# LoRA residual kernel on one Trainium2 core: the copy of the split product moves from GpSimd to VectorE

## The reference

```
B_sel = B[adapter_ids]
A_sel = A[adapter_ids]
Bx  = einsum('bni,bri->bnr', x, B_sel)
out = einsum('bnr,bor->bno', Bx, A_sel)
return x + out
```

## Time and profile before

| what | value |
|---|---|
| median of 3 runs | 96.18 us (95.92 to 96.72) |
| profiled execution | 96.29 us, its span 94.4 us |
| mean granted TensorE clock in it | 0.945 of full |
| moved by DMA | 34.83 MB, mean 369 GB/s |

### The profile page before, as it was taken

How to read it: one execution, slowest core, us unless ns; L and a number is a source line. 1 busy time by engine, 2 the same in 40 slices (tenths; PEclk the granted TensorE clock), 3 DMA queues, 4 the chain that set the end, 5 groups by cost and what they waited for, 6 DMA issues and landing times.

```text
span 94.4 us, 3723 instructions
## 1 busy us (share of the span) xinstructions
PE 81.5 (86%) x1472; PEld 64.5 (68%) x1472; DVE 58.4 (62%) x105; ACT 53.1 (56%) x138; POOL 67.1 (71%) x152
## 2 busy tenths in 40 slices
PE   3994999999999999899999999999989999652800
PEld 3993998787786768587877787777767877440400
DVE  0009541219696949396969677685857695949760
ACT  2219687985747475657667676757556757110000
POOL 6003906379798999979797979797979798986000
PEclk9999999999999999999999999999999999975555
DMA  1999999999999999999999999999999998664676
GB/s 19 305 294 394 419 417 408 408 408 412 401 413 406 408 403 403 410 412 403 408 413 408 419 403 415 417 412 415 417 410 419 410 380 327 271 266 198 247 318 252
DMA packets 11202, 34.83 MB, mean 369 GB/s; under 512 B 2866, under 2 KB 2866, under 8 KB 11186
## 3 DMA queue, kind: packets, MB, share of 16 engines
q1 hardware_dynamic: 11040, 34.08, 91.7%
q10 hardware_dynamic: 146, 0.52, 1.6%
HBM read 17.83 MB, written 16.78 MB: 367 GB/s over the span
## 4 chain that ended last, share of the span: by engine, by line
PE 69%; POOL 9%; DMA 7%; issue 5%; DVE 4%; POOLq 2%; DVEq 1%
PE t_bank L221 31%; PE bx_bank L234 18%; PE y_banks L254 16%; POOL a_duo L162 7%; DMA x_all<-in_A 7%; PE y_banks L212 4%; DVE x_all L363 1%; DVE x_all L341 1%; POOL b_duo L151 1%; DVEq L43 1%; DVE x_all L338 1%; DVE x_all L344 1%; POOL bx_parts L169 1%; POOLq L43 0%; POOLq L162 0%
## 5 line engine op out<-in xcount | busy, mean ns | idle before, releaser
L363 DVE TENSOR_TENSOR x_all<-y_banks,x_all 128x1024 f32<-128x1024 f32 x32 | 39.1, 1224 | 18.7 <-PE y_banks L254 18.2
L301 ACT COPY x_t<-t_bank 128x512 f32<-128x512 f32 x64 | 34.4, 591 | 19.5 <-PE t_bank L221 19.5
L162 POOL CAST a_duo<-a_table 128x512 fp32r x64 | 36.6, 609 | 3.4 <-ACT a_table L306 3.2
L221 PE MATMUL t_bank<-ident,x_all 128*128 128x128 f32 x256 | 34.9, 279 | 1.3 <-DMA x_all<-in_x 1.2
L221 PEld LDWEIGHTS t_bank<-ident,x_all 128*128 128x128 f32 x256 | 27.5, 141 | 7.8 <-issue 4.9
L151 POOL COPY b_duo<-b_table 128x256 f32 x64 | 23.2, 403 | 11.1 <-ACT b_table L287 6.2
L254 PE MATMUL y_banks<-a_duo,bx_parts 64*128 64x512 f32 x128 | 20.8, 445 | 4.0 <-POOL bx_parts L169 3.5
L234 PE MATMUL bx_bank<-x_t,b_duo 128*32 128x64 f32 x1024 | 21.7, 222 | 1.1 <-issue 0.6
L234 PEld LDWEIGHTS bx_bank<-x_t,b_duo 128*32 128x32 f32 x1024 | 16.2, 109 | 7.1 <-issue 6.2
L254 PEld LDWEIGHTS y_banks<-a_duo,bx_parts 64*128 64x128 f32 x128 | 12.0, 197 | 7.5 <-issue 3.5
L355 DVE TENSOR_TENSOR bx_parts<-bx_bank,bx_parts 32x64 fp32r<-32x64 f32 x64 | 14.0, 219 | 4.8 <-ACT bx_parts L316 3.7
(11 more groups left out here) (13 smaller groups left out, 7.4 us busy)
## 6 DMA issues: line engine op xcount, KB each, us to landing
out_y<-x_all SPq DMA_DIRECT2D x32, 512.0 KB, 12.4
x_all<-in_x SPq DMA_DIRECT2D x15, 1024.0 KB, 18.8
x_all<-in_x SPq DMA_DIRECT2D x2, 512.0 KB, 6.0
x_all<-in_B ACTq DMA_DIRECT2D x1, 512.0 KB, 4.1
x_all<-in_A SPq DMA_DIRECT2D x1, 512.0 KB, 6.2
id_row<-in_ids ACTq DMA_DIRECT2D x1, 0.2 KB
```

The lines of the kernel that those rows point to most:

```text
L162: last = nc.gpsimd.tensor_copy(a_duo[duo % 2][:, k, :], a_table[:, bass.ds(adapters[k] * BANK, BANK)])
L221: last = nc.tensor.transpose(t_bank[unit % 2][:, c * P:(c + 1) * P], x_all[:, 2 * duo + tile, at:at + P], ident[:, :])
L301: nc.scalar.copy(x_t[duo % 2][:, half * HALF:(half + 1) * HALF, tile, :], t_bank[unit % 2][:, :].rearrange("p (c n) -> p c n", c=HALF)).th ...
L363: nc.vector.tensor_tensor(here, y_banks[tile][:, :], here, ALU.add).then_inc(y_drained, 1)
```

## The change

double_parts is no longer an instruction of GpSimd but of VectorE. There it stands directly behind split_rest of the same duo and ahead of add_x of tile 1, with a wait for rest_done of that duo. Its operands are the same. GpSimd's waits on parts_done and a_gathered go away with it; PE's wait on parts_done in up() stays.

```diff
@@ gpsimd: gather_b @@
                 if duo >= 2:
                     pool.wait_ge(bx_done, duo - 1)
-                    pool.wait_ge(parts_done, duo - 1)
@@ gpsimd: gather_a @@
                 if duo >= 2:
                     pool.wait_ge(y_filled, 2 * (duo - 1))
-                    pool.wait_ge(parts_done, duo)
...
-            def double_parts(duo):
-                pool.wait_ge(rest_done, duo + 1)
-                pool.wait_ge(a_gathered, duo + 1)
-                nc.gpsimd.tensor_copy(own_tokens(duo, K_UP, 2 * K_UP),
-                                      own_tokens(duo, 0, K_UP)).then_inc(parts_done, 1)
...
                 gather_a(duo, here)
-                double_parts(duo)
@@ vector @@
+            def double_parts(duo):
+                dve.wait_ge(rest_done, duo + 1)
+                nc.vector.tensor_copy(own_tokens(duo, K_UP, 2 * K_UP),
+                                      own_tokens(duo, 0, K_UP)).then_inc(parts_done, 1)
...
             split_rest(0)
+            double_parts(0)
             for duo in range(1, DUOS):
                 add_x(duo - 1, 0)
                 split_rest(duo)
+                double_parts(duo)
                 add_x(duo - 1, 1)
```

## The result

The changed kernel takes 95.68 us at the median of 18 runs (94.71 to 97.1) against 96.17 of before; ratio 0.9927, 95% interval 0.9898 to 0.9955. Timed twice more it gave 0.9898 (0.9827 to 0.9969) and 0.9894 (0.9852 to 0.9936). So it is faster by 0.7 to 1.1%, about 0.7 to 1.0 us, and not by the forecast 1.46. By the line of 1% that the prediction drew, the first ratio, 0.9927, is no change (chance 0.30) and not faster (chance 0.60). Some executions are over 1.5% longer than the fastest of their kernel: ratios leave them out, medians and ranges don't, and the profiles of middle_only, after_half_stores and act_double_again are of such an execution. The profiled execution took 95.48 us, its span 93.5 (before 96.29 and 94.4).

What follows compares the result with a forecast made beforehand. No engine is full; order decides, with GpSimd's 4.57 us turn holding PE's 4.34. 0.50 + 0.15 + 0.87 - 0.06 = 1.46 off 96.29 gives 94.8 us; own range 94.0 to 95.3, stated range 94.0 to 96.6.

Steps and rivals of the forecast that it cites:

- the line of 1%: Least change told from none, 0.96 us: faster below 95.2 us (0.60), slower above 97.1 (0.10), same between (0.30).
- GpSimd's turn of 4.57 against PE's 4.34: Duo loop: GpSimd loses 0.23 us a turn and then holds PE; without the copy its turn is about 4.0.
- The two turns held by GpSimd: Middle turns of 4.58 and 4.60 us, where PE waits for GpSimd's copy, fall to 4.34 each: 0.50 us gained.
- U12 to U13: From PE's first weight load of up(12) to that of up(13): 4.49 us before, 0.15 gained.
- The third rival: PE's stops "issue" inside down() grow 0.8 us in all and add in full: 95.6 us, no change; chance 0.15.
- U13 to U14: From PE's first weight load of up(13) to that of up(14): 4.42 us falls to 3.55, 0.87 gained.
- The copy at 0.31 + 0.2: VectorE's new copy per duo: 0.31 us alone, plus 0.2 for disturbance by GpSimd's gathers running beside it.
- Slack of 0.37: Middle turns: add_x tile 1, behind the new copy, still ends 0.37 us before PE needs it, covering the 0.2.
- The one-gather rival: VectorE's copy waits for the running gather each time, 0.41 to 0.57 us: 95.3 to 96.6 us; chance 0.15.
- The batch rival: VectorE's copy waits 0.96 us behind all four a_duo gathers: about 99.5 us, slower; chance 0.10.
- From U14 on nothing changes: Tail from PE's first weight load of up(14): 0.06 us lost up to add_x(14,0), then nothing; clock left at 0.53.
- The low end of the range: Own range's 94.0 us: copy at 0.22 and 0.08 for the unknowns, and some of PE's holds "issue" gone.

Runs made afterwards that it cites:

- middle_only: Changed kernel with the last two copies back on GpSimd, so VectorE copies for duos 0 to 13 only; ratio 0.9898 to the kernel before.
- after_half_stores: Changed kernel with each tile's store writing only its first 512 columns, half of the output left out; 94.08 us, ratio 0.9713.
- act_double_again: Second timing of the version with the copy on ScalarE instead of VectorE, beside the changed kernel; median 95.50 us, ratio 0.9855 to the kernel before.

## Why the prediction was right in its mechanism and too large in its sum

- *GpSimd's turn of 4.57 against PE's 4.34 makes the lag:* right. After, GpSimd waits for PE in 13 turns; taking its gathers away instead of the copy has the same effect.
- *The two turns held by GpSimd, 0.50, and U12 to U13, 0.15:* this is the step that failed: 0.65 was counted in full, and U0 to U13 changed by +0.08. The holds by GpSimd went (turns 8 and 9 lost 0.36, U12 to U13 0.14), but PE's hold in down(12) took 0.29 back, and the one in down(4) grew by 0.23. The third rival, "PE's own holds take it", is what happened: the three holds are longer by 0.6 in all, where it had 0.8. It added longer holds to the time as if they were independent. The point that it missed is that such a hold swallows what is won between its place and the one before it, so the wait for GpSimd ahead of up(10) had hidden part of it.
- *U13 to U14, 0.87:* right in size, 1.07. The 0.2 between them is the 0.2 that I added for gathers beside the copy: duo 14's copy took 0.29.
- *The copy at 0.31 + 0.2:* 0.29 + 0.24 in the middle. Right.
- *Slack of 0.37 covers it:* right, 0.1 left. The one-gather rival had the mechanism: the copy waits for the gather that runs beside it (last section). But it had 0.4 for the wait, and 0.24 was measured, so the slack covered it. The batch rival had 0.96; by its own formula it comes to about 99.7 and not 99.5, a slip that changes nothing.
- *From U14 on nothing changes:* within 0.1. Leaving the time as it was in spite of the clock was right too: PE ran at the full clock there and only 0.09 was gained.
- *The low end of the range:* no. I let it come from holds that might go. In no profile with full stores did the third hold go, and in the three of the changed kernel none did.

Luck has a part in the total. The profiled execution gained 0.81. From U0 to the last addition's end it gained 1.1, and 1.1 and 1.4 in the two further profiles of the changed kernel. The start took 0.36 of it and the end, behind the last addition, gave 0.18 back. One profile alone understates the gain by that.

What is not settled: why the hold in down(4) grew. It is 0.28 before, 0.29 with only the end changed, 0.28 and 0.27 with few gathers, and 0.48 to 0.51 in the five profiles with 24 warm-ups in which DVE copies beside gathers in the middle; with the copy on ScalarE it is 0.38 and 0.44. So it is longest with that overlap. By what way isn't shown.

## What to carry to other kernels

Before a stall is counted as gain, look for the next stop behind it that has another cause: a transfer, or the engine's own instructions. Ask also from where that stop counts its time. Here it ends some 6.4 us after PE passed a fixed place, so it swallowed the gain behind that place and left the gain ahead of it. What is won behind the last such stop counts in full; here only the last two copies moved gave 0.7%, against 0.7 to 1.1% for all sixteen. Two engines on one resource are priced well from the one place in the trace where they already meet. Slack is spent in the order of the waiting engine's own work: once that engine has no idle time, its sum is the turn.

## What the runs showed of the hardware that was not expected

PE stops for its own instructions: three times while the 16 DMA engines are full, 0.3 to 0.9 us each, 2.2 to 2.7 us behind the start of a 16 KB packet on the instruction queue. For the third stop that packet starts 4.0 to 4.3 us after PE passed the fixed place before, against 0.8 and 1.2 with half of the stores, where the stop is gone.

GpSimd and VectorE at one port: DVE's copy of 0.29 us, begun at 46.87 beside a gather that runs from 46.64 to 47.25, ends at 47.40, and the gather behind takes 0.67 instead of 0.61. At 82.67, 0.14 us before the recorded end of a gather, it takes 0.29. Single instructions of the middle turn after, from the timeline:

```profile
46.64 0.61 POOL L160 CAST a_duo<-a_table 128x512 fp32r x1
46.87 0.53 DVE L353 CAST bx_parts<-bx_parts 64x256 fp32r<-64x256 f32 x1
47.20 0.67 POOL L160 CAST a_duo<-a_table 128x512 fp32r x1
```

All fifteen copies of this profile that meet a gather end 0.14 to 0.16 us behind its recorded end, whether they began 0.13 or 0.39 ahead of it. With two copies it is the same: begun 0.08 to 0.25 us into a gather, the first takes 0.68 to 0.51. Sharing the port in parts would not end them at one fixed point; a wait for the running gather does. By the rule of the Trainium skill that the prediction quotes ("SBUF — State Buffer", section "SBUF: two separate sides") the trace agrees: the copy waits for one whole instruction, and not for the batch. It can also miss its turn: in two turns with two copies it began 0.02 before a gather's recorded end, when the next had already started, and waited for that one too:

```profile
47.48 0.72 DVE L354 CAST bx_parts<-bx_parts 64x256 fp32r<-64x256 f32 x1
```
